# C's rows of the selective scan loaded four states at a time

## The reference

```python
def step(h, inp):
    x_t, dt_t, B_t, C_t = inp
    dA = jnp.exp(A[None] * dt_t[..., None])
    dB = (1.0 - dA) / (A[None] + 1e-08) * B_t[:, None, :]
    h = jnp.clip(dA * h + dB * x_t[..., None], -10.0, 10.0)
    y_t = jnp.sum(C_t[:, None, :] * h, -1) + D_param * x_t
    return (h, y_t)
h0 = jnp.zeros((B, Di, N), x.dtype)                  # B=2, Di=1024, N=16
_, ys = jax.lax.scan(step, h0, xs)                   # over 4096 positions
y = jnp.swapaxes(ys, 0, 1) * jax.nn.silu(z)
return y @ W_out.T
```

## Time and profile before

| | us |
|---|---|
| median of 3 runs | 4360.01 |
| lowest and highest run | 4350.95, 4363.68 |
| the profiled execution | 4355.76 |
| its span in the trace | 4353.9 |
| its scan stage, 1053 to 3467 in the trace | 2414 |

### The profile page before, as it was taken

The page is one execution under the profiler, slowest core; times in us unless marked ns, Lnnn a source line. Parts: engine busy times, 40 slices in busy tenths (PEclk is TensorE's granted clock), DMA queues, the critical chain, the costliest instruction groups (busy, mean ns, idle before and its releaser), DMA issues. The chain is left out here.

```text
span 4353.9 us, 48879 instructions
## 1 busy us (share of the span) xinstructions
PE 4164.5 (96%) x14186; PEld 2462.8 (57%) x14186; DVE 3663.8 (84%) x4288; ACT 3174.8 (73%) x5825; POOL 3102.1 (71%) x1546
## 2 busy tenths in 40 slices
PE   8999999995999999999999999999999869999999
PEld 6777777772444444444444444444444348888887
DVE  7888888884999999999999999999999854444443
ACT  5666666665999999999999999999999712111111
POOL 1110111002999999999999999999999857777772
PEclk9999999997999999999999999999999979999999
DMA  5777776657566657666765666576566365555550
GB/s 174 220 221 206 225 234 222 205 183 216 159 183 187 182 156 195 187 166 167 194 188 155 185 185 181 157 195 185 161 177 184 111 221 174 160 179 181 173 168 30
DMA packets 617005, 787.32 MB, mean 181 GB/s; under 512 B 116748, under 2 KB 344220, under 8 KB 616224
## 3 DMA queue, kind: packets, MB, share of 16 engines
q1 hardware_dynamic: 608288, 767.41, 60.8%
q10 hardware_dynamic: 8448, 16.78, 1.0%
HBM read 541.14 MB, written 244.85 MB: 181 GB/s over the span
## 5 line engine op out<-in xcount | busy, mean ns | idle before, releaser
L985 POOL TENSOR_TENSOR q<-g,cc 128x1024 f32<-128x1024 f32 x1024 | 2395.8, 2374 | 129.7 <-DVE g L1124 122.6
L1124 DVE TENSOR_TENSOR_SCAN g<-dd,carry,ps_a 128x512 f32<-128x512 f32 x2048 | 2400.3, 1256 | 32.7 <-ACT ps_a L1007 28.1
L1064 PE MATMUL ps_y<-q,w_s 128*128 128x512 f32 x4096 | 2102.0, 594 | 10.3 <-DMA w_s<-w_d 5.4
L1007 ACT ACTIVATE ps_a<-dt_s,small 128x512 f32<-128x512 f32 x2048 | 1502.0, 733 | 5.4 <-DVE g L1124 5.4
L996 ACT ACTIVATE dd<-ps_d 128x512 f32<-128x512 f32 x2048 | 1288.3, 629 | 65.6 <-PE ps_d L1051 42.8
L1051 PE MATMUL ps_d<-dm,xk 99*128 99x512 f32 x2048 | 1129.4, 552 | 64.1 <-DMA dm<-band_d 26.3
L1051 PEld LDWEIGHTS ps_d<-dm,xk 99*128 99x128 f32 x2048 | 384.1, 188 | 1210.7 <-ACT dd L996 944.6
L1064 PEld LDWEIGHTS ps_y<-q,w_s 128*128 128x128 f32 x4096 | 773.5, 191 | 189.8 <-issue 56.5
L334 POOL TENSOR_TENSOR xnt_lo<-xnt_f,xnt_hi 128x512 fp32r<-128x512 f32 x62 | 81.0, 1307 | 580.2 <-ACT xnt_hi L371 580.2
L504 PE MATMUL ps_r_f<-xnt_hi,w_hi 128*128 128x512 f32 x1024 | 420.0, 410 | 3.8 <-DVE w_lo L687 3.8
L504 PE MATMUL ps_r_f<-xnt_lo,w_hi 128*128 128x512 f32 x1024 | 402.3, 393 | 0.0
(11 more groups left out here) (166 smaller groups left out, 4422.4 us busy)
## 6 DMA issues: line engine op xcount, KB each, us to landing
w_s<-w_d SPq DMA_DIRECT2D x256, 512.0 KB, 3.7
xk<-xt_d SPq DMA_DIRECT2D x768, 132.0 KB
xt_d<-xt_f SPq DMA_DIRECT2D x256, 256.0 KB, 3.0
cc<-c_d SPq DMA_DIRECT2D x128, 512.0 KB, 11.4
dm<-band_d SPq DMA_DIRECT2D x192, 264.0 KB
xs_d<-xs_f SPq DMA_DIRECT2D x128, 256.0 KB, 2.5
zs_d<-zs_f SPq DMA_DIRECT2D x128, 256.0 KB, 3.0
dt_d<-lg_f SPq DMA_DIRECT2D x32, 1024.0 KB, 6.7
```

The source lines that it names most:

```text
L985: pool.tensor_tensor(q[:, s % QB:s % QB + 2, :], g[:, s % GB:s % GB + 2, :], rows, ALU.mult).then_inc(s_q, 2)
L1007: act.activation(ps_a[:, s % AB, :], dt[:, blk % DTB, :], ACT.Exp, scale=small[:, blk % MD, S_A + n:S_A + n + 1]).then_inc(s_a, 1)
L1064: pe.matmul(ps_y[:, blk % 2, :], w[:, half % WB, at:at + P], q[:, s % QB, :], start=(n == 0), stop=(n == NS - 1)).then_inc(s_n, 1)
L1124: dve.tensor_tensor_scan(g[:, s % GB, :], dd[:, m % 2, n, :], ps_a[:, s % AB, :], carry[:, m, n:n + 1], ALU.add, ALU.mult).then_inc(s_g, 1)
```

## The change

`CN` goes from 2 to 4 and `CR` from 10 to 5. A load then brings four rows (a group, 1 MB, 8 KB in one piece per partition) and the ring has 5 places of four rows, 20 rows as before. There are 64 loads of C in place of 128. GpSimd still multiplies two states at once (`at` picks the half of the group) and, in a chunk's first block, waits for the whole group before the first of its two products.

```diff
--- before.py
+++ after.py
@@ -782,7 +782,7 @@
     LEAD = 3
     LAG = 6
     HALF = NBLK // 2
-    XB, DTB, CN, WB, CR = 3, 3, 2, 3, 10
+    XB, DTB, CN, WB, CR = 3, 3, 4, 3, 5
     FINISH_AT = 10
     PIECES = 4
     EACH = NBLK // PIECES
@@ -903,14 +903,12 @@
                 load_dt(0)
                 load_dt(1)
                 load_c(0, 0)
-                load_c(0, 1)
                 load_x(1, 0)
                 sp.wait_ge(s_dps, HALF)
                 load_x(1, 1)
                 load_w(0, 0)
                 load_w(0, 1)
-                load_c(0, 2)
-                load_c(0, 3)
+                load_c(0, 1)
                 load_ahead(0)
                 load_prev(0)
                 for blk in range(BLOCKS):
@@ -923,16 +921,14 @@
                     load_dt(blk + 2)
                     load_prev(blk + 1)
                     if m == 0:
-                        for i in range(4 if ch == 0 else 8, 8):
+                        for i in range(2 if ch == 0 else NS // CN, NS // CN):
                             load_c(ch, i)
                     if m == 1 and more:
                         if ch > 0:
                             sp.wait_ge(s_dm[PIECES - 1], 48 * ch)
                         fill_band(ch + 1)
-                    if m in (3, 4):
-                        load_c(ch + 1, m - 3)
-                    if m == MD - 1:
-                        load_c(ch + 1, 2)
+                    if m == 3:
+                        load_c(ch + 1, 0)
                     if blk > 0:
                         sp.wait_ge(s_n, NS * blk)
                     load_w(blk + 1, 0)
@@ -941,15 +937,13 @@
                         sp.wait_ge(s_dps, made + EACH)
                         load_b(ch + 1, 0)
                     if m == MD - 1:
-                        load_c(ch + 1, 3)
-                        load_c(ch + 1, 4)
+                        load_c(ch + 1, 1)
                     if blk + 1 < BLOCKS:
                         sp.wait_ge(s_dps, made + HALF)
                     if m == MD - 2 and more:
                         load_b(ch + 1, 1)
                     load_x(blk + 2, 1)
                     if m == MD - 1 and more:
-                        load_c(ch + 1, 5)
                         load_ahead(ch + 1)
                     if blk > 0:
                         store_y(blk - 1)
@@ -958,11 +952,12 @@
                             sp.wait_ge(s_dps, made + EACH * (i + 1))
                             load_b(ch + 1, i)
                     if m == MD - 1:
-                        load_c(ch + 1, 6)
-                        load_c(ch + 1, 7)
+                        load_c(ch + 1, 2)
                     if blk + 1 < BLOCKS:
                         sp.wait_ge(s_n, NS * blk + NS // 2)
                     load_w(blk + 1, 1)
+                    if m == MD - 1:
+                        load_c(ch + 1, 3)
                 store_y(BLOCKS - 1)
                 for e in range(2):
                     sp.wait_ge(s_yo[e], 16 * BLOCKS // 2)
@@ -978,7 +973,8 @@
                     pair = ch * (NS // CN) + n // CN
                     if s % STEPS < NS:
                         pool.wait_ge(s_cc[pair % CR], 16 * (pair // CR) + 16)
-                    rows = cc[:, CN * (pair % CR):CN * (pair % CR) + CN, :]
+                    at = CN * (pair % CR) + n % CN
+                    rows = cc[:, at:at + 2, :]
                     pool.wait_ge(s_g, s + 2)
                     if s >= QB:
                         pool.wait_ge(s_n, s - QB + 2)
```

## The result

| | before | changed |
|---|---|---|
| median of 7 runs each, us | 4358.84 | 4388.04 |
| lowest and highest | 4350.95, 4363.68 | 4383.09, 4406.9 |
| ratio, 95% interval | | 1.0076, 1.0061 to 1.0092 |
| span of the profiled execution | 4353.9 | 4382.2 |
| VectorE from its first scan to its last | 2408.3 | 2436.7 |

The change costs 29 us, 0.8%. (The ratio is that of the runs; the two medians alone give 1.0067, inside its interval.) The forecast was 4362, with a range up to 4372. The whole difference lies in the scan: 2436.7 - 2408.3 = 28.4 us, the same as between the two spans, 28.3.

What follows compares the result with a forecast made beforehand. VectorE was taken to set the pace in the scan. The start's +2.1 us and the turns' 0, added to the median 4360.0, gave 4362 us; range 4352 to 4372.

Steps and rivals of the forecast that it cites:

- the turns: The 15 passages from one chunk to the next in the scan: loads still land in time, cost 0.
- a load lands when all bytes ahead of it are through: At chunk turns, DMA engines limit loads; counting bytes left 2.3 us to spare for the third group, 1.0 for the fourth.
- What moves forward: At turns, `xk` behind group 1 and the second `w_s` have fewer bytes ahead: up to -2.4 us, left out of the sum.
- 1.0 + 2.3 = 3.3 us: At an ordinary turn, 1.0 us to spare for the fourth group plus GpSimd's 2.3 us of free lag.
- The free lag of 2.3 us: In the scan, GpSimd may be 2.3 us behind VectorE at no cost; what goes beyond is passed on.
- each us of lateness costs 1 us: At a chunk turn, lateness beyond the cover of 3.3 us costs VectorE its full length at that turn.
- The start: Scan's first block: groups land with their second pairs, GpSimd's pair 4 starts later, +2.1 us (bounds 0 and +2.8).
- Rival 1: Loads of C in the scan: larger loads are faster loads, time 4355 us; chance 0.12.
- Rival 2: Fourth group too late at every turn because 8 KB pieces move slower: about 4380 to 4402 us; chance 0.09.
- Its point: At turns, VectorE pays once 8 KB pieces are 1.1 us per MB slower, 5.45 us per MB against 4.35.
- its own formula: For x us per MB slower, the fourth group is 3x late; each of 15 turns costs 3x less 3.3 us.

Runs made afterwards that it cites:

- the coarser wait alone: Kernel before, loads and order untouched; only GpSimd waits for both pairs of a group ahead of the first one's product: 4355.68 us against 4354.47, ratio 1.0002.

## Why the prediction was wrong

**The size of the time was missed by one term, the turns.** It said "So all turns cost nothing". They cost some 25 us more than before (27.3 against 2.7). The step under it was "a load lands when all bytes ahead of it are through", with the pace of today's bytes. Bytes were counted rightly and their pace was not: the same 5.4 MB took 23.6 us in place of 21.1. Two loads of 512 KB per group, otherwise the change, needed 21.7 and lost about 3 us in the scan.

**The party that waits was the wrong one.** "What moves forward" counted the `xk` behind group 1 and the second `w_s`, and both did come sooner. It did not ask what stands behind the fourth group. That is the next block's first half of `xk`, and the same bytes ahead of it do not mean the same time. TensorE waited 0.2 to 1.0 us there in 13 of the 15 turns before. After the change up to 2.5 us of waiting lost nothing, and 2.9 already stopped VectorE for 1.45. The cover of "1.0 + 2.3 = 3.3 us" was GpSimd's alone; TensorE's was not in the sum. In five of the nine turns that lost time GpSimd stayed within its 2.3 us, so TensorE's wait is what is left there; in four GpSimd was beyond it too.

**The free lag of 2.3 us was right** for GpSimd, to the tenth, as the point where the cost begins. That "each us of lateness costs 1 us" beyond it held in six turns of fifteen; in the others 1.3 to 2.5 us came on top. **The start** was right in its waits (4.68 and 3.55 us ahead of pairs 2 and 4 with the coarser wait alone) and, partly by luck, in its size, +2.1. Another 2 us came in the changed kernel, where group 1 landed 11.3 us after its issue and the prediction took 10.4.

**Rival 1** took the loads of `W_in` as the pattern for 8 KB pieces. Those loads read 128 rows that all differ, and the loads of C 16; the prediction named "the one source row that eight partitions read" and then let it stand. With 32 rows the same pieces of C ran at 24.0 bytes per ns and nothing was lost, so the source had to be weighed before the size of the piece. The rule cited there (the Trainium skill, "DMA: Bandwidth & Descriptors", "Rules for kernel authors", 1 MiB or more per DMA) holds in this kernel only as "no worse" and only with 32 source rows; with 16 the load of 1 MB was the slower one, 14.5 against 15.9 bytes per ns.

**Rival 2** had the direction and the place, the last loads of every turn, and 0.09. Its point was too far out: it asked for 1.1 us more per MB, and 2.5 us over three groups, 0.8 per MB, were enough, because TensorE's cover was smaller and some turns were later than the median (the fourth group landed up to 20.2 us after the first scan). And the cost is not only the lateness beyond a threshold. Where VectorE stops in block 1, a second stop of up to 1.45 us at block 2 comes with it. That is why 27 us came at the turns where its own formula gives nothing.

## What to carry to other kernels

When a row is broadcast to 128 partitions from DRAM, look at how many different rows one load reads: here 16 rows gave some two thirds of the pace that 32 gave. Ask of every load that grows what stands behind it in the queue and how much its reader may be late, for each reader and not only for the one that uses the load; here 2.5 us more in a turn of 21 were within GpSimd's cover at an ordinary turn, and beyond TensorE's in nine of fifteen. Where three orders of the same loads name three different waits and none is faster, look at the pace of the bytes before trying a fourth: here the DMA engines were busy 96 to 98% of the turn, and what helped was bytes that moved faster.

## What the runs showed of the hardware that was not expected

- Pieces read by a load from 16 rows of DRAM ran at 14.5 to 16.3 bytes per ns and engine, from 32 rows at 22.3 to 24.0, from 64 at 23.9; loads of 128 rows that all differ (`w_s`) were slowed beside them, to 15.4 beside loads of 1 MB from 16 rows against 20.7 beside loads from 32; copies 516 KB apart were as slow as 512 KB apart.
- A load of 1 MB in 8 KB pieces from 16 rows was slower (14.5) than the same bytes in two loads for 64 partitions (16.3) or in two loads of 4 KB pieces (16.1).
- One store that writes 32 copies of 32 KB per chunk from 16 partitions cost 64 us over 16 chunks in `front`; two stores of 16 copies at different places cost nothing that can be told from the spread of the start of the scan (1050 to 1058 us).
